# Two multiplies of the adaptive softmax moved to VectorE for the first pairs, its polynomial factored, and a new order table

## The reference, cut to what matters

```python
original_probs = softmax(logits)
entropy = sum(-original_probs * log(original_probs + 1e-09))
e2 = entropy * entropy
poly = P0*e2*e2 + P1*e2*entropy + P2*e2 + P3*entropy + P4
beta = where(entropy > 0.5, maximum(poly, 1.0), 1.0)
return softmax(logits * beta)
```

## Time and profile before

| | us |
|---|---|
| median of 3 runs | 1454.74 (1453.48 to 1459.05) |
| the profiled execution | 1466.06 |
| its span in the profile | 1463.2 |
| PE, VectorE, ScalarE, POOL busy | 1312.7, 779.7, 689.0, 536.1 |
| mean granted clock of TensorE | 0.963 |

### The profile page before, as it was taken

How to read it: one execution, slowest core, us unless ns; L and a number is a source line. 1 busy time by engine, 2 the same in 40 slices (tenths; PEclk the granted TensorE clock), 3 DMA queues, 4 the chain that set the end, 5 groups by cost and what they waited for, 6 DMA issues and landing times. The chain is left out here.

```text
span 1463.2 us, 23121 instructions
## 1 busy us (share of the span) xinstructions
PE 1312.7 (90%) x8464; PEld 989.9 (68%) x8464; DVE 779.7 (53%) x1791; ACT 689.0 (47%) x1254; POOL 536.1 (37%) x777
## 2 busy tenths in 40 slices
PE   9899999988999999896667989989989779999996
PEld 7576767757999999894334665656656545666664
DVE  4876868673111111113656687977776645433332
ACT  6454747552222222222447687768777445222221
POOL 2123130402000000006878887887867033322222
PEclk9999999999999999998869999999999989999998
DMA  9673563903877777713000001000010634322221
GB/s 352 252 200 106 123 166 106 230 12 124 292 264 264 262 267 280 279 48 98 19 1 5 20 29 33 20 29 20 0 48 16 243 97 136 60 39 41 44 39 11
DMA packets 70686, 171.00 MB, mean 117 GB/s; under 512 B 8508, under 2 KB 47425, under 8 KB 60464
## 3 DMA queue, kind: packets, MB, share of 16 engines
q1 hardware_dynamic: 54944, 144.39, 30.9%
q0 software_dynamic: 10224, 16.09, 5.3%
q10 hardware_dynamic: 5408, 9.04, 1.7%
HBM read 123.11 MB, written 48.07 MB: 117 GB/s over the span
## 5 line engine op out<-in xcount | busy, mean ns | idle before, releaser
L1187 ACT ACTIVATE b_ht<-ps,b_b 128x154 f32<-128x154 f32 x256 | 85.4, 387 | 205.8 <-PE ps L1154 189.5
L1202 DVE TENSOR_SCALAR b_yt<-ps,b_b 128x154 f32<-128x154 f32 x64 | 21.2, 373 | 244.0 <-PE ps L1167 244.0
L2309 POOL DMA_INDIRECT experts<-ye,gidx_all x32 | 32.1, 1002 | 325.2 <-SPq L1093 314.6
L2384 PE MATMUL ps<-experts,d_xt 128*128 x312 | 147.1, 594 | 1.2 <-ACT d_xt L2440 0.8
L1154 PE MATMUL ps<-b_xet,ring 128*128 128x154 f32 x1024 | 143.7, 298 | 3.7 <-ACT b_ht L1187 3.7
L1154 PEld LDWEIGHTS ps<-b_xet,ring 128*128 128x128 f32 x1024 | 138.3, 192 | 3.9 <-issue 3.8
L1167 PE MATMUL ps<-b_ht,ring 128*128 128x154 f32 x1024 | 139.7, 294 | 0.4 <-DVE b_yt L1202 0.4
L1167 PEld LDWEIGHTS ps<-b_ht,ring 128*128 128x128 f32 x1024 | 136.3, 189 | 0.6 <-issue 0.6
L2526 POOL DMA_INDIRECT out_dram<-d_yd,d_to x39 | 60.6, 1554 | 158.5 <-DVE d_yd L2498 151.2
L1523 DVE TENSOR_REDUCE c_mx<-ps 128x8 f32<-128x1024 f32 x64 | 77.8, 1215 | 63.8 <-PE ps L1468 63.3
L1486 PE MATMUL ps<-cf,experts 128*128 128x128 f32 x512 | 73.3, 290 | 24.8 <-DVE experts L1529 12.6
(11 more groups left out here) (336 smaller groups left out, 2839.0 us busy)
## 6 DMA issues: line engine op xcount, KB each, us to landing
ring<-in_w SPq DMA_DIRECT2D x64, 1024.0 KB, 5.4
xd<-zero SPq DMA_DIRECT2D x6, 3120.0 KB, 25.9
a_kp<-in_ctx_k SPq DMA_DIRECT2D x8, 1024.0 KB
experts<-in_wd SPq DMA_DIRECT2D x1, 7424.0 KB
d_xd<-xd SPq DMA_DIRECT2D x39, 130.0 KB, 2.1
xe<-zero SPq DMA_DIRECT2D x1, 4928.0 KB, 33.2
b_xe<-xe SPq DMA_DIRECT2D x32, 154.0 KB
ye<-b_ye ACTq DMA_DIRECT2D x32, 154.0 KB
```

The lines of the kernel that those rows point to most:

```text
L1187: r = a.activation(ht[:, e % 2, m, :], ps[:, b, CAP * (m % 2):CAP * (m % 2) + CAP], ACT.Gelu, bias=b1[:, e, m:m + 1])
L2384: m = pe.matmul(ps[:, b, :], xt[:, j % 2, k, :], w13[:, bass.ds(e, 1), f:f + F1], start=(k == 0), stop=(k == KD - 1))
```

## The change

For pairs 0 and 1 the product "pr" is issued by VectorE, at the place that the new table gives, instead of POOL. The polynomial is computed as POLY[0] times the product of two quadratics in h, whose coefficients the host works out from its roots; nine operations take the place of ten. The whole of the table `AT_C` is replaced. Of its some 190 pieces those stand here that are spoken of; the eight numbers are those of pairs 0 to 7.

```diff
@@ -42,6 +42,16 @@
 NEG = -1.0e30
 LN_EXP = "natural_log_exp_and_others"
 POLY = [-0.037, 0.481, -2.3, 4.917, -1.791]
+BY_VECTOR = 2
+
+
+def quadratic_factors(p):
+
+    roots = sorted(np.roots([p[0], -p[1], p[2], -p[3], p[4]]), key=lambda r: (abs(r.imag), r.real))
+    return [(float(-(r + s).real), float((r * s).real)) for r, s in (roots[:2], roots[2:])]
+
+
+FACTORS = quadratic_factors(POLY)
 RING = 4
 NB = 8
 ND = 6
...
-    "xk": (17.2, 131.5, None, None, None, None, None, None),
+    "xk": (3.6, 134.8, None, None, None, None, None, None),
-    "xv": (33.2, 136, None, None, None, None, None, None),
+    "xv": (6.4, 138.3, None, None, None, None, None, None),
-    "xvi": (38.9, 137.9, None, None, None, None, None, None),
+    "xvi": (8.3, 140.2, None, None, None, None, None, None),
-    "comb": (6.4, 10.2, 20.6, 27.1, 40.1, 176.1, 193.9, 231.6),
+    "comb": (9.5, 12.5, 20.6, 28.6, 62.1, 50.6, 99.5, 80.3),
-    "fetch0": (0, 3.8, 11.5, 20.5, 27, 146.6, 157, 202),
+    "fetch0": (0, 1.3, 11.5, 16.7, 28.4, 32.3, 86.7, 68),
-    "pn0": (30.8, 70.3, 111.6, 155, 219.3, 280.7, 337.6, 396),
+    "pn0": (34.8, 66, 105, 157.8, 222, 280.6, 335.3, 392.9),
-    "mx0": (23.6, 56.2, 94, 141, 206.5, 271.2, 329.3, 389.3),
+    "mx0": (25.6, 55.6, 95.5, 149.9, 214.3, 273.4, 327, 384.8),
-    "pr2": (49.8, 93.4, 132.1, 188, 242, 309.6, 357.9, 417.1),
+    "pr2": (52.5, 88.6, 128.3, 193.5, 249.5, 301.8, 356.2, 412.1),
-    "db1": (56.8, 90.1, 136.3, 181.8, 252.7, 303.4, 360.2, 419.4),
+    "db1": (52.2, 81.5, 126.4, 191.5, 243.3, 304.1, 362.7, 424.8),
-    "tr0": (51.6, 86.9, 133.3, 183.6, 243.7, 305.8, 358.9, 418.6),
+    "tr0": (48, 88.9, 127, 185.5, 245.7, 303.3, 358.3, 415.8),
-    "tr3": (75, 115.6, 171.8, 230.5, 294.4, 348.5, 407.9, 441.3),
+    "tr3": (76.5, 117.5, 174.8, 235.3, 293, 347.8, 405.1, 446.6),
-    "res": (87.7, 142.7, 191.8, 249, 309, 363, 419.4, 466.3),
+    "res": (89.9, 147.5, 196.6, 249.1, 308.9, 362.5, 419.2, 462.1),
-    "xd": (99.7, 154.8, 207.8, 261.1, 322.9, 377.9, 432.5, 476.7),
+    "xd": (101.4, 159.7, 208.8, 262.8, 325, 375.3, 430.2, 472.5),
-    "t0": (12.5, 25.9, 79.5, 122.6, 194, 260.1, 316.6, 378),
+    "t0": (15.2, 27.9, 81.2, 126.2, 196.5, 261.9, 313.2, 372.4),
-    "t5": (178.7, 238.1, 299.6, 353.7, 416, 460.1, 504.9, 527),
+    "t5": (179.3, 240.2, 298.3, 352.8, 411.9, 454.2, 497.2, 523.3),
...
@@ -1606,7 +1616,7 @@
         upto_keys = upto_rotary + KD * GT + 4 * KD * GT
         m4, z4 = sb("m4", [P, GS]), sb("z4", [P, GS])
         zz, en, po = ([sb("%s%d" % (name, u), [P, NU]) for u in range(len(UNITS))] for name in ("zz", "en", "po"))
-        gt = [[sb("%s%d" % (name, u), [P, NU]) for name in ("sq_h", "g_h", "odd")] for u in range(len(UNITS))]
+        gt = [[sb("%s%d" % (name, u), [P, NU]) for name in ("square", "other", "chosen")] for u in range(len(UNITS))]
         x_rot, x_rms = [sb("x_rot%d" % n, [P, GS, D]) for n in range(2)], sb("x_rms", [P, GS, D])
         kr = sb("kr", [2 * 4 * HD, GT])
         rows, ss = [sb("rows%d" % n, [P, GS, D + 4]) for n in range(2)], sb("ss", [P, GS])
@@ -1770,6 +1780,7 @@
             return unit
 
         def temperature_vector(g):
+
             at = tick(g)
 
             def unit(u):
@@ -1779,6 +1790,10 @@
                 v.tensor_reduce(zz[u][:, :], e[:, :, :], AX, ALU.add).then_inc(*c.dv.up())
                 v.wait_ge(*c.dv.now())
                 v.reciprocal(zz[u][:, :], zz[u][:, :]).then_inc(*zr.up())
+                if g < BY_VECTOR:
+                    yield at("pr", u)
+                    v.wait_ge(*ln.at(g, u))
+                    v.tensor_tensor(e[:, :, :], e[:, :, :], lnp[u % 2][:, :, :], ALU.mult).then_inc(*pr.up())
                 yield at("hr", u)
                 v.wait_ge(*pr.at(g, u))
                 v.tensor_reduce(h, e[:, :, :], AX, ALU.add).then_inc(*hr.up())
@@ -1790,29 +1805,29 @@
 
             def unit(u):
                 e, l, d = ent[u % 2][:, :, :], lnp[u % 2][:, :, :], one.d[u][:, :, :]
-                h, p, (sq_h, g_h, odd) = en[u][:, :], po[u][:, :], (x[:, :] for x in gt[u])
+                h, p, (square, other, chosen) = en[u][:, :], po[u][:, :], (x[:, :] for x in gt[u])
                 yield at("pn", u)
                 pool.wait_ge(*zr.at(g, u))
                 pool.tensor_tensor(e, e, wide(zz[u]), ALU.mult).then_inc(*pn.up())
-                yield at("pr", u)
-                pool.wait_ge(*ln.at(g, u))
-                pool.tensor_tensor(e, e, l, ALU.mult).then_inc(*pr.up())
+                if g >= BY_VECTOR:
+                    yield at("pr", u)
+                    pool.wait_ge(*ln.at(g, u))
+                    if g == BY_VECTOR and u == 0:
+                        pool.wait_ge(*pr.at(g - 1))
+                    pool.tensor_tensor(e, e, l, ALU.mult).then_inc(*pr.up())
                 yield at("po", u)
                 pool.wait_ge(*hr.at(g, u))
-                pool.tensor_tensor(sq_h, h, h, ALU.mult).then_inc(*c.po.up())
-                pool.tensor_scalar(g_h, h, -0.5, None, ALU.is_lt)
+                pool.tensor_tensor(square, h, h, ALU.mult)
+                pool.tensor_scalar(p, h, *FACTORS[0], ALU.mult, ALU.add)
+                pool.tensor_scalar(other, h, *FACTORS[1], ALU.mult, ALU.add).then_inc(*c.po.up())
+                pool.tensor_scalar(chosen, h, -0.5, POLY[0], ALU.is_lt, ALU.mult)
                 pool.wait_ge(*c.po.now())
-                pool.tensor_scalar(p, sq_h, POLY[0], POLY[2], ALU.mult, ALU.add)
-                pool.tensor_scalar(odd, sq_h, -POLY[1], -POLY[3], ALU.mult, ALU.add).then_inc(*c.po.up())
+                pool.tensor_tensor(p, p, square, ALU.add)
+                pool.tensor_tensor(other, other, square, ALU.add).then_inc(*c.po.up())
                 pool.wait_ge(*c.po.now())
-                pool.tensor_tensor(p, p, sq_h, ALU.mult)
-                pool.tensor_tensor(odd, odd, h, ALU.mult).then_inc(*c.po.up())
+                pool.tensor_tensor(p, p, other, ALU.mult).then_inc(*c.po.up())
                 pool.wait_ge(*c.po.now())
-                pool.tensor_tensor(p, p, odd, ALU.add).then_inc(*c.po.up())
-                pool.wait_ge(*c.po.now())
-                pool.tensor_scalar(p, p, POLY[4], None, ALU.add).then_inc(*c.po.up())
-                pool.wait_ge(*c.po.now())
-                pool.tensor_tensor(p, p, g_h, ALU.mult).then_inc(*c.po.up())
+                pool.tensor_tensor(p, p, chosen, ALU.mult).then_inc(*c.po.up())
                 pool.wait_ge(*c.po.now())
                 pool.tensor_scalar(p, p, 1.0, None, ALU.max).then_inc(*be.up())
                 yield at("db", u)
```

More of the change, by code:

```diff
@@ L1297 @@
 AT_C = {
[87 rows of a table removed]
-    "xadd": (185.7, 244.3, 305.3, 362.1, 425.5, 465.6, 510.8, 531.1), "rtp": (187, 245.6, 306.6, 363.4, 433, 467.3, 513.6, 532.4),
[3 rows of a table removed]
-    "count": (None, 254.6, None, 374.9, None, 476.6, 522.3, 539.6), "gap": (None, 255, None, 372.8, None, 476.7, 522.3, 539.6),
-    "wta": (None, 257.5, None, 376.3, None, 478.1, 522.8, 540.1), "weights": (None, 259.1, None, 379.9, None, 485.5, 524.1, 541.4),
[4 rows of a table removed]
[87 rows of a table added]
+    "xadd": (185, 245.3, 307.4, 359.5, 416.8, 461.5, 501.3, 527.4), "rtp": (186.3, 246.6, 306.4, 358.5, 420.4, 463.2, 502.6, 528.7),
[3 rows of a table added]
+    "gap": (None, 256.3, None, 368.3, None, 472.6, 511.3, 535.8), "count": (None, 256.3, None, 367.5, None, 472.4, 514.1, 535.8),
+    "wta": (None, 259.2, None, 369.9, None, 474, 518.5, 536.3), "weights": (None, 260.8, None, 371.5, None, 481.4, 519.8, 537.6),
[4 rows of a table added]
 }
```

## The result

The changed kernel took 1467.04 us (median of nine executions, 1461.97 to 1472.67), the kernel before 1461.63 (nine, 1453.48 to 1464.72): ratio 1.0055, 95% interval 1.0038 to 1.0071. Forecast was no change within 0.5%, with 1453.5 us between 1442 and 1466. It became slightly slower. The rest is the sign: -1.2 us was forecast and +5.4 came.

A forecast was written before the change was run, and what follows sets the result against it. PE bounds the middle (89% busy, 762 to 1160 us); both ends are thin, partly at 1.2 GHz. Terms -3.7 + 0.9 + 1.6 = -1.2 us give 1453.5 us against the median 1454.74; range 1442 to 1466.

The forecast's parts named there:

- the sign: Whole program: terms sum to -1.2 us, counted as no change within 0.5%; chance of this case 0.42.
- The table's term: Order table, gathers, multiplies and polynomial together: -3.7 us, by pair 7's earlier planned end; bounds 0 and -7.7.
- The start: Beginning of pair 0: keys and values ahead of first combine put turn at 689.3; charged +0.9 us, between 0 and +1.7.
- the slack: Behind pair 0's start: some of the 1.7 us behind the plan is absorbed further on, so half is charged.
- the zero of 672.4: Offset from old table to trace, laid on pair 0's first normalization: planned at 30.8, begun at 703.20.
- Contention: First 100 us: VectorE's products and POOL hold each other, three meetings; +1.6 us, ends 0 and +12.3.
- the queued row maximum: VectorE, first loop: pair 1's row maximum queues behind pair 0's product, which waits 1.6 us for POOL.
- The code's own terms: POOL loses 18.9 us of multiplies, VectorE gains 9.8 at 1.22 each; polynomial 0.28 us less per unit.
- Rival 1: First loop no longer feels the slow clock, VectorE fills its waits: 8.7 us back, 1444.8 us; chance 0.20 with like gains.
- Rival 2: VectorE bounds first 100 us, waits and stretched combines lose 12.3 us: +9.5, 1464.2 us; chance 0.22 with like losses.
- Rival 3: Packed middle: freed POOL time brings nothing, table's 3.7 lost, start and one wait remain; +2.5, 1457.2 us; chance 0.16.
- The base: Median of the kernel before that the forecast started from, 1454.74 us, three executions; its profiled execution took 1466.06.

The follow-up runs named there:

- C: Against before: idle matmuls in pair 0 added 0.9945; to both code parts, old table 0.9956; to whole change with sums for products 1.0006; old/new table mixed 1.0311.
- D: Against before: whole change again 1.0009; with row maximum ahead of product 1.0012; with old start and idle matmuls 0.9955; polynomial, old table, sums for products 0.9933.
- the sum: Whole change with VectorE's eight products replaced by one-input sums over the same tile, entropies of pairs 0 and 1 left out, against before: 0.9995.
- A: Against before: new table alone 1.0153; polynomial alone, old table 0.9978; multiplies alone, old table 1.0016; whole change with pair 0's keys and values at old places 1.0033.
- B: Against before: both code parts, old table 0.9953; whole change with late gathers 1.0054, with one-input sums for products 0.9995, with idle matmuls in pair 0 0.9971.

## Why the prediction was wrong

**The table's term failed.** The prediction read the new table as a plan that would hold as the old one did, and took -3.7 us with bounds of 0 and -7.7. Both bounds forbade a loss. The table alone cost 1.5%; beside the code it was drawn for, about 0.8% (1.0033 against 0.9953 from different comparisons; 1.0006 against 0.9956, so 0.5%, inside C, with sums for the products). A plan's times are what its author assumed of clock and waits. Nothing in the trace of before said that a different order would be kept as closely, and the old table already lost 19.5 us by the first tile. A quarter more of that turns the sign, and that is what came (24.4); the range of the term should have reached as far above nothing as below.

**The start was mis-sized.** Its steps were right: the combine came at 682.43 (forecast 683.4), the turn at 689.01 (689.3). (The prediction's own terms add up to 683.0, not 683.4.) But "pn0" came at 710.21, not near 707: 3.0 us behind the plan instead of 0.9, and C shows that it is not made up. The step that failed is the slack. In before the turn came at 680.89, 4.0 us ahead of its planned 684.9, and "pn0" on time, for turn to "pn0" took 22.3 us where the old table has 18.3; the zero of 672.4, laid on "pn0", hid that. There was nothing to absorb a late turn: counted from the stretch's beginning the turn came 8.9 us later and "pn0" 7.8, of which the plan had 4.0. The way between them was no slower than before (21.2 us, clock 0.92 in both); in the execution of D, at the low clock, it took 25.2.

**Contention went by the row and was under-priced in number, over-priced in effect.** Forecast: three meetings, one of them costing 1.6 us. In the trace three products took 2.09, 2.56 and 2.78 us, 4.0 us above eight times 1.2, and POOL's operations from 690 to 800 us took some 6.5 us more, by an estimate that sums each against its usual time: the product at 773.79 held the normalization that began 0.16 us behind it to 2.77 us instead of 1.89. The product of 737.66 began 0.20 us behind POOL's multiply and ended 1.08 us behind its end. This is the rule of the Trainium skill, SBUF — State Buffer, "Who interferes with whom", in both directions, and this trace agrees: whichever began second was held. But the whole of it is worth 0.1 to 0.6% of the time at most (0.9995 with the sum against 1.0009 to 1.0055), and the queued row maximum nothing. In the trace of D no product was held at all, so the number of meetings is not set by the table, as the forecast had it; a shift of some microseconds in the queues undoes them.

**The code's own terms held.** The polynomial brought 0.37 us per unit (0.28 forecast) and 0.22% of the time in A, which the prediction had left inside the table's term. The multiplies alone brought nothing (1.0016), and both together 0.47% in B. The two results of A multiply to 0.9994; the 0.4% between that and 0.9953 is at the edge of what different comparisons can tell. Products that met nothing took 1.17 to 1.33 us (1.22 forecast).

**The rivals.** Rival 1 named the right reserve (8.7 us; 8.2 in the loop by C) and the wrong remedy: PE was no busier in the loop (65.2 of the 100 us from 700 on, 67.5 before), and the time at 1.2 GHz there rose from some 42 to some 56 us, by the clocks of 0.79 and 0.72. Rival 2's sign came, but not its picture: the first tile came at 1220.18, not after 1225, and VectorE was 80% busy from 736 to 767 us, not 90. Rival 3, the table's gain lost and the start kept, is nearest: +2.5 us, where the two traces differ by 1.2 at the first tile and the medians by 5.4. It lacked the further loss at the thin end (clock 0.80 instead of 0.86 in the earlier trace rows), which the prediction named only among the odds of rival 2.

**The base.** 6.9 us of the miss are that three executions of before stood for it. That the profiled one took 1466.06 was a warning: executions of the kernel before took from 1450.03 to 1475.28 us over all comparisons.

**Open.** That the table costs is shown; how its loss splits between start, slow clock and held products wasn't settled. They overlap, and the remedies don't add: the idle matmuls bring 0.55% to before and, against both code parts of B (0.9953), nothing to those (0.9956, another comparison); the start undone is worth nothing alone (1.0033) and at most 0.2% beside them (0.9955 against 0.9971). Open too is why one pair of kernels gives ratios 0.46% apart on different occasions. The slow start seen in D is part of the scatter (4.3 us by "pn0", 4.1 by the first tile, of one trace), and another part lies ahead of the stretch; what decides whether the clock falls there no run shows.

## What to carry to other kernels

Measure a new order and a change of code apart: here the code gained up to 0.5% and the new order gave more than that back. Read a hand-written order as a wish, and price a new one by how much of the old one was lost and where. Lay the plan on the trace from the beginning of the stretch and not from a piece inside it, or a lead ahead of that piece will look like slack. Idle matmuls in a thin stretch were the cheaper gain here. Compare traces from the point at which the changed code begins. Make the base of a forecast of a few microseconds from more than three runs.

## What was not expected of the hardware

- A gather's issue on POOL was held too: at 714.11 it took 1.79 us instead of 0.95, having begun 0.39 us behind a product of 1.33 us on VectorE. All twelve issues from 670 to 850 us, over all traces, that began behind a running product took 1.78 to 1.95 us; the thirteen that began first took 0.96 to 0.97, and the product that began during them wasn't held (1.17 to 1.24). The Trainium skill, SBUF — State Buffer, "Who interferes with whom", infers that issuing descriptors isn't in the way of such an instruction; these rows speak against it. Both kinds in the trace of D:

```profile
720.36 1.32 DVE L1796 TENSOR_TENSOR experts<-experts 128x1024 f32<-128x1024 f32 x1
720.75 1.79 POOL L2324 DMA_INDIRECT experts<-ye,gidx_all  x1
...
722.85 0.96 POOL L2324 DMA_INDIRECT experts<-ye,gidx_all  x1 [0.30 <-issue]
722.86 1.24 DVE L1796 TENSOR_TENSOR experts<-experts 128x1024 f32<-128x1024 f32 x1
```

- Even a two-column operation is held: POOL's shift of norm statistics took 1.20 us at 739.33 beside the product of 737.66, and 0.24 elsewhere.
- One kernel, in two executions, ran from 689 to 697 us, behind the same matmuls, at a granted clock of 1.00 and of 0.50: 1.99 against 3.78 us for the same eight matmuls.
- The same kernel's ratio to another differed by 0.46% between occasions, with intervals of 0.2% each.
